# Cross-attention block: wholly masked queries through a 78th key, and four output projections as three f16 products

## The chip, the cores and the metric

The kernel runs on 1 core of one Trainium2 chip. The metric is the device time of one execution in microseconds (us); of several executions the median counts.

## The reference

Four sequences of 1024 queries attend to 77 context rows each, with 16 heads of 16 elements. Keys with mask 1 are excluded. The rest of the block is the output projection, the residual and a layer norm.

```python
q = split_heads(x @ W_Q.T); k = split_heads(ctx @ W_K.T); v = split_heads(ctx @ W_V.T)
scores = einsum('bhqd,bhkd->bhqk', q, k) / sqrt(16)
scores = where(mask[:, None] == 1, -1e9, scores)     # mask: (4, 1024, 77)
p = softmax(scores, axis=-1)
out = concat_heads(einsum('bhqk,bhkd->bhqd', p, v)) @ W_O.T + x
return (out - mean(out)) * rsqrt(var(out) + 1e-5) * gamma + beta
```

x is (4, 1024, 256), ctx (4, 77, 256), everything is f32 and the mask int32. Where all 77 keys of a query are masked, all scores are the same -1e9, so the softmax gives every key 1/77 and the query gets the mean of the values.

## The kernel before

**Tiles.** The 4096 queries are cut into 8 blocks of 512 (`BLOCKS`, `N`), two for each sequence. Columns hold queries. Heads go in 8 pairs; a block has 8 steps s = 0..7, one pair each. Each engine has its own program, all orders are written out by hand, and semaphores tie them.

**Scores as one matmul.** For block m the tile `R[m % 3]` has 126 partitions for each head: 77 rows of the mask (`eq16`: 61440 where the key is masked), 48 rows of q as f16 in three parts (high, low, high again), and one row with the negated maximum of the head. The tile `kb` holds the other side: a negated identity for the mask (`copy_tail`, L688), k in parts (high, high, low), and a row of ones. `scores` (L876) multiplies all 126 rows, two heads a step; `max_unit` (L845) multiplies the first 125 for the maxima, in 12 units a block (heads in groups of 6, 6 and 4, four tiles of 128 queries), which `reduce_max` (L631) reduces on DVE. `turn_max` transposes the 128x16 maxima on PE (L859), ACT copies them (L516) and a DMA (L520) writes them as one row of R. So the maxima of block n+1 are done in steps 0 to 3 of block n, those of n+2 are begun in steps 5 to 7 (`UNITS_LATE`, `UNITS_EARLY`); in block 0 units of blocks 0, 1 and 2 stand in the steps (`OWN_FIRST`, `NEXT_FIRST`, `EARLY_FIRST`).

**Wholly masked queries.** `count` (L804) sums the 77 mask rows of a block with one f16 matmul of ones into `work_ps`. ACT makes a flag of it (`nf`, L480: 1 if not all are masked, else 0), and `q_scale` (L620, DVE) multiplies the projected q by the flag on its way from PSUM into `q32`, so a wholly masked query has equal scores for all keys.

**q.** `project_q` (L824) projects a half of a block (128 of 256 outputs, 512 queries) in f32 into `work_ps`, at steps 1 and 3 of block n for block n+3. Then come `q_scale`, `q_hi` (L487, ACT: q as f16), `q_lo` (L344 on POOL; L613 on DVE for block 0: the rest as f16), and on SP `load_q` (L260 for the high part twice, L262 for the low part), which moves the halves into rows of R. `q_hi` waits until the previous block's parts have left `q16`. The mask comes as int32 by `load_mask_i`, becomes f16 by `eq` (L339 on POOL, L597 on DVE for blocks 0 and 1), and is spread over 8 heads by `load_mask` (L251, 616 KB for half of the heads); in blocks 0 and 1 DVE spreads it (L694).

**Values and output.** `exp` (L526, ACT) writes the probabilities of two heads. `values` (L885) multiplies four heads by v and by a column of ones, at steps 2, 4 and 6 and at step 0 of the next block. DVE turns the result (`turn`: L639, and the reciprocal of the sums, L641), POOL divides (`norm`, L351), DVE turns back (`turn_back`, L647). `project_out` (L895) projects in f32 the two halves of block n-1 at steps 5 and 7 of block n (steps 3 and 5 for n = 6), 4 matmuls a half, which the profile shows as 8 passes. DVE adds x (`residual`, L653), takes the statistics (L659, L664), POOL makes 1/std and the shift (`moments`, L360 to L365), ACT applies them (`apply`, L531) and POOL multiplies by gamma and adds beta (L372, L378). `work_ps`, one bank, serves count, project_q and project_out in turn; each waits for the reader of the one before.

**Orders around the change.** ACT at step 0: exp, nf(n+3); at 2 and 4: exp, q_hi(n+3); at step 4 (5 in block 0) turn_max(n+1) behind exp. DVE at step 2 and 4: q_scale(n+3), then reductions, turn, reductions. POOL in a block: norm, gamma and beta of block n-3, q_lo, moments(n-2), eq(n+4). SP in a pass n: mask and q of block n+2, second half; mask_i and x_t of block n+4; x; mask and q of block n+3, first half; the store of block n-3. SP waits in order, so each DMA of it is behind those before. w_o is loaded from ACT's queue behind q_hi(0, 0) (L547).

## Time and profile before

| what | value |
|---|---|
| median of 3 runs | 182.79 us (181.10 to 183.29) |
| the profiled execution's own time | 183.17 us |
| its span in the profile | 181.4 us |
| PE busy | 160.0 us (88%) |
| DVE busy | 136.5 us (75%) |
| ACT busy | 100.5 us (55%) |
| POOL busy | 95.8 us (53%) |
| mean granted TensorE clock | 0.988 |

The span is what lies between the first and the last instruction of the profiled execution; 1.8 us of its own time lie around it. Busy times count each engine's own instructions, which may overlap waits of others. Matmul ends are modelled, so two neighbouring PE rows can overlap by some 0.2 us; the distance of their starts is the better measure. The chain of waits goes back from the last instruction to what released it, step by step. Lines are those of the kernel before.

### The profile page before, as it was taken

The numbers are of one execution on the slowest core, as the hardware profiler recorded it, in microseconds if no ns is written. First come the engines' busy times: TensorE is split into PE (matmuls) and PEld (weight loads), VectorE is DVE, ScalarE is ACT, GpSimd is POOL, SyncE is SP. The second block draws the span as 40 slices with busy tenths as digits, with TensorE's granted clock in tenths as the row PEclk, the third lists the DMA queues.
The fourth block names the chain that finished last, engine by engine and source line by source line (L and its number), as shares of the span: only waits on it lengthen the run. The fifth ranks groups of instructions, "written<-read, shape, count | busy, mean of one in ns | idle before, by whom it ended". The sixth has DMA issues, their size and how long they took to land.

```text
span 181.4 us, 3507 instructions
## 1 busy us (share of the span) xinstructions
PE 160.0 (88%) x1224; PEld 87.0 (48%) x1224; DVE 136.5 (75%) x303; ACT 100.5 (55%) x134; POOL 95.8 (53%) x119
## 2 busy tenths in 40 slices
PE   7798878889699999999999999999899799799830
PEld 7555544343344554455545554554356364164520
DVE  0858757684978499778977897789989985758991
ACT  3224155563475655558755875586667458796400
POOL 7000750330743451249576957664954675895692
PEclk9999999999999999999999999999999999999995
DMA  5959958768767977872797575656541024011205
GB/s 174 350 144 169 260 86 222 208 143 246 195 173 239 268 223 222 266 195 48 212 264 188 179 209 133 190 159 197 148 173 64 4 107 129 0 59 61 116 0 231
DMA packets 21829, 30.17 MB, mean 166 GB/s; under 512 B 3436, under 2 KB 17356, under 8 KB 21812
## 3 DMA queue, kind: packets, MB, share of 16 engines
q1 hardware_dynamic: 20692, 28.19, 54.8%
q10 hardware_dynamic: 1120, 1.76, 2.9%
q8 instruction: 10, 0.16, 0.4%
q14 instruction: 7, 0.06, 0.1%
HBM read 11.28 MB, written 4.19 MB: 85 GB/s over the span
## 4 chain that ended last, share of the span: by engine, by line
PE 57%; DVE 11%; DMA 9%; issue 7%; POOL 7%; ACT 6%; SPq 1%; POOLq 0%; ACTq 0%; DVEq 0%
PE pv_ps L885 13%; PE work_ps L824 11%; PE work_ps L895 11%; PE scores_ps L876 9%; PE max_ps L845 8%; DMA x_t<-in_x_cols 4%; DVE neg_max L631 4%; DMA R<-neg_max_t 3%; DVE ctx_q L639 2%; DMA R<-q 2%; PE scores_ps L824 2%; POOL y L372 2%; ACT probs L526 2%; POOL y L378 1%; DVE first_max L631 1%
## 5 line engine op out<-in xcount | busy, mean ns | idle before, releaser
L526 ACT ACTIVATE probs<-scores_ps 77x1024 f32<-77x1024 f32 x60 | 60.5, 1017 | 43.7 <-PE scores_ps L876 38.4
L631 DVE TENSOR_REDUCE neg_max<-max_ps 128x6 f16<-128x462 f32 (+1 forms) x84 | 45.4, 565 | 11.9 <-PE max_ps L845 11.8
L845 PEld LDWEIGHTS max_ps<-kb,R 125*128 125x128 f16 x512 | 26.2, 98 | 34.4 <-DVE neg_max L631 17.8
L344 POOL TENSOR_TENSOR q<-q 128x512 f16<-128x512 f32 x14 | 16.2, 1155 | 49.5 <-ACT q L487 49.5
L876 PE MATMUL scores_ps<-R,kb 126*77 126x512 f16 x120 | 36.1, 384 | 1.0 <-DMA R<-neg_max_t 1.0
L845 PE MATMUL max_ps<-kb,R 125*128 125x77 f16 x512 | 31.9, 199 | 4.3 <-DVE neg_max L631 3.3
L885 PE MATMUL pv_ps<-probs,v_all 77*32 77x512 f32 x248 | 33.0, 604 | 2.6 <-ACT probs L526 1.5
L351 POOL TENSOR_TENSOR ctx_n<-ctx_q,rden 128x256 f32<-128x256 f32 x31 | 19.4, 627 | 23.9 <-DVE rden L641 23.6
L639 DVE STREAM_TRANSPOSE ctx_q<-pv_ps 128x512 f32<-128x512 f32 x31 | 22.0, 709 | 9.8 <-PE pv_ps L885 9.4
L895 PE MATMUL work_ps<-wo_t,ctx_e 128*128 128x256 f32 x112 | 27.0, 384 | 0.1
L824 PE MATMUL work_ps<-x_t,wq_t 128*128 128x512 f32 x48 | 23.6, 614 | 0.4
L895 PEld LDWEIGHTS work_ps<-wo_t,ctx_e 128*128 128x128 f32 x112 | 20.7, 190 | 3.6 <-issue 0.6
L372 POOL TENSOR_TENSOR y<-y,gamma_sb 128x512 f32<-128x512 f32 x14 | 17.8, 1272 | 3.0 <-ACT y L531 3.0
L531 ACT ACTIVATE y<-y,shift,rstd 128x256 f32<-128x256 f32 x28 | 15.1, 589 | 3.3 <-POOL shift L365 3.3
L378 POOL TENSOR_TENSOR y<-y,beta_sb 128x512 f32<-128x512 f32 x12 | 15.2, 1271 | 0.0
L876 PEld LDWEIGHTS scores_ps<-R,kb 126*77 126x77 f16 x120 | 9.9, 117 | 9.5 <-ACT probs L526 4.1
L487 ACT ACTIVATE q<-q 128x512 f16<-128x512 f32 x16 | 9.9, 620 | 7.5 <-DVE q L620 5.3
L339 POOL TENSOR_SCALAR eq<-mask_i 77x512 f16<-77x512 int32 x6 | 11.6, 1928 | 1.6 <-DMA mask_i<-in_mask_cols 1.2
L653 DVE TENSOR_TENSOR y<-work_ps,y 128x512 f32<-128x512 f32 x14 | 9.5, 680 | 2.7 <-PE work_ps L895 2.7
L647 DVE STREAM_TRANSPOSE ctx_e<-ctx_n 128x512 f32<-128x512 f32 x15 | 10.5, 701 | 1.1 <-POOL ctx_n L351 1.0
L824 PEld LDWEIGHTS work_ps<-x_t,wq_t 128*128 128x128 f32 x48 | 8.2, 190 | 6.6 <-issue 5.7
L659 DVE BATCH_NORM_STATS2 bn<-y 128x6 f32<-128x256 f32 x28 | 9.9, 397 | 0.0
(88 smaller groups left out, 149.0 us busy)
## 6 DMA issues: line engine op xcount, KB each, us to landing
R<-eq SPq DMA_DIRECT2D x12, 616.0 KB
R<-q SPq DMA_DIRECT2D x48, 128.0 KB
x_t<-in_x_cols SPq DMA_DIRECT2D x8, 512.0 KB, 5.4
y<-in_x SPq DMA_DIRECT2D x8, 512.0 KB, 4.6
out<-y SPq DMA_DIRECT2D x7, 512.0 KB, 2.6
mask_i<-in_mask_cols SPq DMA_DIRECT2D x8, 154.0 KB
out<-y ACTq DMA_DIRECT2D x2, 256.0 KB, 2.0
kb<-k SPq DMA_DIRECT2D x12, 38.5 KB, 2.9
```

The source lines that it names most:

```text
L344: nc.gpsimd.tensor_tensor(q16[:, e, 1, :], q32[:, e, :], q16[:, e, 0, :], ALU.subtract).then_inc(q_low, 1)
L351: nc.gpsimd.tensor_tensor(ctx_n[:, v, :, u * DK:(u + 1) * DK], ctx_q[:, t % 2, :, 0:DK], rden[:, t % 2, :].unsqueeze(2).to_broadcast([P, C ...
L372: nc.gpsimd.tensor_tensor(rows, rows, gamma_sb[:, :].unsqueeze(1).to_broadcast([P, 2, D]), ALU.mult).then_inc(y_gamma, 1)
L378: nc.gpsimd.tensor_tensor(rows, rows, beta_sb[:, :].unsqueeze(1).to_broadcast([P, 2, D]), ALU.add).then_inc(y_beta, 1)
L526: nc.scalar.activation(probs[:, s, :, :], scores_ps[scores_buffer(PAIRS * n + s)[0]][0:KEYS, :, :], ACT.Exp).then_inc(exp_done, 1)
L631: nc.vector.tensor_reduce(to[:, t, lo:hi], max_ps[u % 2][:, 0:(hi - lo) * KEYS].rearrange("p (h k) -> p h k", k=KEYS), AX.X, ALU.max, nega ...
L639: nc.vector.transpose(ctx_q[:, t % 2, :, :], pv_ps[:, :]).then_inc(pv_turned, 1)
L824: last = nc.tensor.matmul(bank, wq_t[:, t, e * P:(e + 1) * P], x_t[m % X_RING][:, t, :], start=(t == 0), stop=(t == HALVES - 1))
L845: last = nc.tensor.matmul(max_ps[u % 2][:, (h - lo) * KEYS:(h - lo + 1) * KEYS], R[m % R_RING][0:MAX_ROW, h, t * P:(t + 1) * P], kb[0:MAX_ ...
L876: last = nc.tensor.matmul(scores_ps[buffer][0:KEYS, i, :], kb[:, 2 * s + i, n // PER_BATCH, :], R[n % R_RING][:, 2 * s + i, :], start=True ...
L885: last = nc.tensor.matmul(pv_ps[32 * j:32 * (j + 1), :], v_all[:, n // PER_BATCH, 4 * t + j, :], probs[:, 2 * t + j // 2, j % 2, :], start ...
L895: last = nc.tensor.matmul(work_ps[:, i * D:(i + 1) * D], ctx_e[n % 2][:, v, q0:q0 + P], wo_t[:, v, :], start=(v == 0), stop=(v == HALVES - 1))
```

## The change

A 78th column of `kb` (`COLS = KEYS + 1`) stands for a key whose value is the mean of the values: its context row is the mean of the 77 others (`sum_ctx`, `mean_ctx` on DVE), so project_v gives its value. Its score comes from the mask's rows: each masked key adds 256, and a new row of R that is all ones (`ONE_ROW`) takes away 77 x 256 - 64. With all keys masked it stands 64 above zero, else at least 192 below. Its k is zero. The maxima are still taken over 77 keys. R and `kb` get 127 rows, exp writes 78 partitions.

- PE: the 8 counts go. project_q now waits for q_low (or out_ready) where it waited for the flag or q_scaled. project_v waits for ctx_mean. project_out of blocks 0 to 3 makes 12 f16 products a half (high x high, high x low, low x high for each of 2 halves of K and 2 tiles) instead of 4 f32 ones and waits for c_low instead of ctx_e_ready.
- ACT: the 8 flags go. q_hi reads PSUM as soon as q is projected, and stands before exp at steps 2 and 4 (2, 4, 6 in block 0; before exp(1, 0) for the last) instead of behind it. New: c_hi(n-1, v) behind exp at steps 0 and 2 of n = 1 to 4; w_hi behind exp(0, 5), ahead of turn_max(1). At the start ACT issues the high parts of k and q for the second half.
- DVE: q_scale goes; every q_lo comes here, reading PSUM, behind the first reductions of steps 2 and 4. New: sum_ctx, two mean_ctx, w_lo at step 7 of block 0, eq_late(n+4) at step 6 of n = 1 to 3 (ahead of the last reductions). residual multiplies by 1/64 for blocks 0 to 3 (w_o is scaled by 64). copy_tail copies a ready f16 tile.
- POOL: all q_lo go, and eq for blocks 5 to 7; eq(4) stands ahead of norm(0, 1). New: c_lo(n-1, v) for n = 1 to 4 behind norm(n-1, 3) and norm(n, 0); in blocks 1 to 4 beta and moments stand later; for block 6 norm(6, 0) moves ahead of both beta, and norm(6, 1) ahead of moments(4). Small memsets at the start.
- SP: w_o is loaded behind load_q(2, 1). At the start two rows of kb and the ones rows of R[0] and R[1] take the place of one row of ones; the ones row of R[2] goes behind the mask of block 2.

```diff
@@ PE
             def project_out(n, half):
                 if half == 0:
-                    pe.wait_ge(ctx_e_ready, HALVES * (n + 1))
+                    if n < OUT_SPLIT:
+                        pe.wait_ge(w_low, 1)
+                        pe.wait_ge(c_low, HALVES * (n + 1))
+                    else:
+                        pe.wait_ge(ctx_e_ready, HALVES * (n + 1))
...
+                        if n < OUT_SPLIT:
+                            for of_c, of_w in [(0, 0), (0, 1), (1, 0)]:
+                                last = nc.tensor.matmul(work_ps[:, i * D:(i + 1) * D], c16[:, v, of_c, q0:q0 + P], wo16[:, of_w, v, :],
+                                                        start=(v == 0 and of_c + of_w == 0), stop=(v == HALVES - 1 and of_c == 1))
...
                     if 1 <= n and n + 3 < N:
-                        if s == 0:
+                        if s == 1:
                             if n >= 2:
                                 pe.wait_ge(out_ready, 2 * (n - 1))
                             else:
-                                pe.wait_ge(q_scaled, 4 * HALVES)
-                            count(n + 3)
-                        if s == 1:
-                            pe.wait_ge(nf_ready, n + 4)
+                                pe.wait_ge(q_low, 4 * HALVES)
                             project_q(n + 3, 0, work_ps[:, :])
                         if s == 3:
-                            pe.wait_ge(q_scaled, HALVES * (n + 3) + 1)
+                            pe.wait_ge(q_low, HALVES * (n + 3) + 1)
                             project_q(n + 3, 1, work_ps[:, :])
@@ ACT
-            def q_hi(m, e):
-                act.wait_ge(q_scaled, HALVES * m + e + 1)
+            def q_hi(m, e, bank):
+                act.wait_ge(q_done, HALVES * m + e + 1)
                 if m > 0:
                     act.wait_ge(s_R[(m - 1) % R_RING][e], loaded_R(m - 1))
-                nc.scalar.activation(q16[:, e, 0, :], q32[:, e, :], ACT.Copy).then_inc(q_high, 1)
+                nc.scalar.activation(q16[:, e, 0, :], bank, ACT.Copy).then_inc(q_high, 1)
+
+            def c_hi(m, v):
+                act.wait_ge(ctx_e_ready, HALVES * m + v + 1)
+                if m > 0:
+                    act.wait_ge(out_done, 2 * m)
+                nc.scalar.activation(c16[:, v, 0, :], ctx_e[m % 2][:, v, :], ACT.Copy).then_inc(c_high, 1)
+
+            def w_hi(w16, w_t, s_w):
+                act.wait_ge(s_w, 16)
+                nc.scalar.activation(w16[:, 0, :, :], w_t[:, :, :], ACT.Copy, scale=WSCALE).then_inc(w_high, 1)
...
             for n in range(N):
                 for s in range(STEPS):
+                    if n == 0 and s in (2, 4, 6):
+                        q_hi(2 + s // 6, s // 2 - 1 if s < 6 else 0, work_ps[:, :])
+                    if n == 1 and s == 0:
+                        q_hi(3, 1, work_ps[:, :])
+                    if n >= 1 and n + 3 < N and s in (2, 4):
+                        q_hi(n + 3, s // 2 - 1, work_ps[:, :])
                     exp(n, s)
                     if n == 0:
                         if s == 1:
                             turn_first_max(2)
-                        if s in (2, 4, 6):
-                            q_hi(2 + s // 6, s // 2 - 1 if s < 6 else 0)
-                        if s == 4:
-                            nf(3)
+                        if s == 5:
+                            w_hi(wo16, wo_t, s_wo)
...
                     if s == nm_at(n) and n + 1 < N:
                         turn_max(n + 1)
@@ DVE
+            def eq_late(m):
+                dve.wait_ge(s_mask[m % 2], 16 * (m // 2 + 1))
+                for e in range(HALVES):
+                    dve.wait_ge(s_R[(m - 2) % R_RING][e], loaded_R(m - 2))
+                nc.vector.tensor_scalar(eq16[m % 2][:, :], mask_i[m % 2][:, :], 1.0, BIG, ALU.is_equal, ALU.mult
+                                        ).then_inc(eq_ready, 1)
...
                     for m, u in before:
                         reduce_max(m, u)
+                    if n == 0 and s in (2, 4, 6):
+                        q_lo(2 + s // 6, s // 2 - 1 if s < 6 else 0, work_ps[:, :])
+                    if n >= 1 and n + 3 < N and s in (2, 4):
+                        q_lo(n + 3, s // 2 - 1, work_ps[:, :])
+                    if n == 0 and s == 7:
+                        w_lo(0, wo16, wo_t)
                     if s == 0 and n >= 1:
                         turn(n - 1, 3)
                     if s in (2, 4, 6):
                         turn(n, s // 2 - 1)
...
+                    if s == 6 and 1 <= n and n + 4 < N:
+                        eq_late(n + 4)
                     for m, u in behind:
                         reduce_max(m, u)
@@ POOL
             norm(N - 3, 3)
             times_gamma(N - 5, 1)
+            norm(N - 2, 0)
             plus_beta(N - 5, 0)
-            norm(N - 2, 0)
             plus_beta(N - 5, 1)
+            norm(N - 2, 1)
             moments(N - 4)
-            norm(N - 2, 1)
             times_gamma(N - 4, 0)
```

## Rows read from the trace of the kernel before

**Rows 1.** Busy time of each engine, from the page (share of the span, instructions)

```profile
PE 160.0 (88%) x1224; PEld 87.0 (48%) x1224; DVE 136.5 (75%) x303; ACT 100.5 (55%) x134; POOL 95.8 (53%) x119
```

**Rows 2.** Windows of two middle blocks: stretch, length, busy us (instructions), clock, DMA, GB/s

```profile
69.40:87.70 18.30, 18.08 (x145) 9.60 (x142) 15.29 (x35) 12.20 (x17) 9.49 (x12) 1.00 0.64 181
87.70:106.00 18.30, 18.08 (x147) 9.62 (x145) 15.30 (x36) 12.22 (x17) 13.28 (x16) 1.00 0.74 209
```

**Rows 3.** Chain of waits, one out projection and what follows: start us, us

```profile
61.78 1.73 PE work_ps L895 x8
63.51 0.23 PE max_ps L845 x6
...
66.16 0.43 PE scores_ps L876 x2
```

**Rows 4.** Chain of waits, count, flag and projection of q in block 2

```profile
70.47 0.34 PE work_ps L804
70.83 0.69 ACT not_full L480
71.57 1.98 PE work_ps L824 x4
```

**Rows 5.** Groups by line and form: count, busy us, mean ns, idle before

```profile
L344 POOL TENSOR_TENSOR q<-q 128x512 f16<-128x512 f32 x14 | 16.2, 1155 | 49.5 <-ACT q L487 49.5
...
L487 ACT ACTIVATE q<-q 128x512 f16<-128x512 f32 x16 | 9.9, 620 | 7.5 <-DVE q L620 5.3 <-DMA R<-q 2.2
...
L620 DVE TENSOR_TENSOR q<-work_ps,not_full 128x512 f32<-128x512 f32 x12 | 8.2, 684 | 1.3 <-PE work_ps L824 1.3
...
L597 DVE TENSOR_SCALAR eq<-mask_i 77x512 f16<-77x512 int32 x2 | 0.8, 418 | 3.4 <-DMA mask_i<-in_mask_cols 3.4
```

**Rows 6.** DVE in order of time: start us, us, idle time before it

```profile
82.06 1.18 DVE L631 TENSOR_REDUCE neg_max<-max_ps 128x6 f16<-128x462 f32 x2 [0.85 <-PE max_ps L845]
```

**Rows 7.** DMA issues: KB each, median us from issue to landing

```profile
wq_t<-in_w_q ACTq DMA_DIRECT2D x1, 256.0 KB, 4.9
...
wo_t<-in_w_o ACTq DMA_DIRECT2D x1, 256.0 KB, 2.6
...
R<-neg_max_t ACTq DMA_DIRECT2D x7, 16.0 KB, 4.7
...
kb<-ones SPq DMA_DIRECT2D x1, 9.6 KB, 7.6
```

**Rows 8.** A DVE copy (ns min/median/max) and a POOL norm beside it

```profile
L688 DVE TENSOR_SCALAR kb<-ident x4: 473/474/798, 4.6 to 47.1; 77x1232 f16<-77x1232 f16 x4
...
47.50 0.86 POOL L351 TENSOR_TENSOR ctx_n<-ctx_q,rden 128x256 f32<-128x256 f32 x1
```

**Rows 9.** Chain of waits at the start: the third DMA of q

```profile
13.06 3.89 DMA R<-q
```

**Rows 10.** Block 0 in order of time, then two pieces of its chain

```profile
31.86 0.61 ACTq L510 DMA_DIRECT2D R<-first_max_t  x1
...
33.02 0.72 DVE L639 STREAM_TRANSPOSE ctx_q<-pv_ps 128x512 f32<-128x512 f32 x1 [0.88 <-PE pv_ps L885]
...
40.30 0.61 SPq L262 DMA_DIRECT2D R<-q  x1
...
43.55 0.59 ACT neg_max_t L516
44.16 5.91 DMA R<-neg_max_t
```

**Rows 11.** The end of block 6 in order of time

```profile
147.73 0.23 POOL L360 TENSOR_SCALAR var_eps<-mean_var 128x4 f32<-128x4 f32 x1
...
149.76 0.62 POOL L351 TENSOR_TENSOR ctx_n<-ctx_q,rden 128x256 f32<-128x256 f32 x1
...
151.01 1.08 ACT L531 ACTIVATE y<-y,shift,rstd 128x256 f32<-128x256 f32 x2
...
154.94 1.07 PE L885 MATMUL pv_ps<-probs,v_all 77*32 77x512 f32 x8 [1.00 <-ACT probs L526]
```

More of the change, by code:

```diff
@@ L30 @@
 CHUNKS = BLOCK // 32
+COLS = KEYS + 1
 Q_ROW = KEYS
 MAX_ROW = Q_ROW + 3 * DK
-ROWS = MAX_ROW + 1
-MASKED = 61440.0
+ONE_ROW = MAX_ROW + 1
+ROWS = ONE_ROW + 1
+BIG = 32768.0
+PER_KEY = 256.0
+WHOLE = 64.0
 KSCALE = 1.0 / float(DK) ** 0.5
@@ L305, in _ @@
                     load_q(n + 2, 1)
+                if n == 0:
+                    sp.dma_start(wo_t[:, :, :], w_o).then_inc(s_wo, 16)
                 if n == 1:
@@ L332, in eq, with c_lo @@
                 pool.wait_ge(s_mask[m % 2], 16 * (m // 2 + 1))
-                pool.wait_ge(count_done, m - 1)
                 if m - 2 < SPREAD:
                     pool.wait_ge(first_mask, HALVES * (m - 1))
-                else:
-                    for e in range(HALVES):
-                        pool.wait_ge(s_R[(m - 2) % R_RING][e], loaded_R(m - 2))
-                nc.gpsimd.tensor_scalar(eq16[m % 2][:, :], mask_i[m % 2][:, :], 1.0, MASKED, ALU.is_equal, ALU.mult
+                nc.gpsimd.tensor_scalar(eq16[m % 2][:, :], mask_i[m % 2][:, :], 1.0, BIG, ALU.is_equal, ALU.mult
                                         ).then_inc(eq_ready, 1)
-            def q_lo(m, e):
-                pool.wait_ge(q_high, HALVES * m + e + 1)
-                nc.gpsimd.tensor_tensor(q16[:, e, 1, :], q32[:, e, :], q16[:, e, 0, :], ALU.subtract).then_inc(q_low, 1)
+            def c_lo(m, v):
+                pool.wait_ge(c_high, HALVES * m + v + 1)
+                nc.gpsimd.tensor_tensor(c16[:, v, 1, :], ctx_e[m % 2][:, v, :], c16[:, v, 0, :], ALU.subtract).then_inc(c_low, 1)
             def norm(m, t):
@@ L705, in _ @@
             spread_mask(0, 1)
-            q_scale(0, 0, q_ps[0][0])
+            sum_ctx()
+            mean_ctx(0)
+            q_lo(0, 0, q_ps[0][0])
             eq(1)
-            q_lo(0, 0)
-            q_scale(0, 1, q_ps[0][1])
-            q_lo(0, 1)
+            q_lo(0, 1, q_ps[0][1])
             spread_mask(1, 0)
-            q_scale(1, 0, q_ps[1][0])
             spread_mask(1, 1)
             k_lo_second()
-            for u in range(TILES):
-                reduce_max(0, u)
+            mean_ctx(1)
+            reduce_max(0, 0)
+            reduce_max(0, 1)
+            q_lo(1, 0, q_ps[1][0])
+            reduce_max(0, 2)
+            reduce_max(0, 3)
             reduce_max(0, TILES)
             reduce_max(0, TILES + 1)
-            q_scale(1, 1, q_ps[1][1])
             reduce_max(0, TILES + 2)
+            q_lo(1, 1, q_ps[1][1])
             reduce_max(0, TILES + 3)
@@ L732, in _ @@
                     if n == 1 and s == 0:
-                        q_scale(3, 1, work_ps[:, :])
+                        q_lo(3, 1, work_ps[:, :])
                     if s == 0 and n >= 2:
                         residual(n - 2, 1)
-                    if s in (2, 4) and 1 <= n and n + 3 < N:
-                        q_scale(n + 3, s // 2 - 1, work_ps[:, :])
                     if s == 6 and 1 <= n < N - 2:
@@ L801, in _ @@
         def _(pe):
-            def count(m):
-                pe.wait_ge(eq_ready, m + 1)
-                nc.tensor.matmul(work_ps[:, :], ones16[:, :], eq16[m % 2][:, :], start=True, stop=True).then_inc(count_done, 1)
             def project_k(p, e):
@@ L936, in _ @@
             max_unit(0, 7)
-            pe.wait_ge(v_ready, 2)
-            count(2)
             pe.wait_ge(first_ready, 1)
             turn_first_max(1)
-            pe.wait_ge(q_scaled, HALVES)
-            pe.wait_ge(tail_ones, 16)
+            pe.wait_ge(q_low, HALVES)
+            pe.wait_ge(s_last_rows, 64)
             for n in range(N - 1):
```

221 lines of the change are left out of this document (116 added, 105 removed).

## The prediction

> **What bounds the kernel now.** I read the page first: PE is busy 88% of the span and DVE 75% [rows 1], of a span of 181.4 us with 1.8 around it. Then the windows of two middle blocks: each takes 18.30 us, PE busy 18.08 of it at a granted clock of 1.00, DVE 15.3, ACT 12.2, POOL 9.5 to 13.3 [rows 2]. So blocks 2 to 4 are bound by TensorE at its full 2.4 GHz, and DVE has 3 us to spare. Then the chain of waits, for the places where PE is not the last link: the start (x_t, q and q's way into R), block 0 (ACT, DVE, and the row of maxima on its way to R) and the end (moments, apply, exponentials). A shorter PE stage pays in the middle; moved work can cost at both ends. Below, n is the block of a loop pass, s its step.
>
> **Middle: out projections.** A half has 8 recorded f32 passes of 256 columns, 1.73 us [rows 3]. It gets 12 f16 products of 256 columns. The nearest rows: two f16 scores of 512 columns in 0.43 us, 0.215 each, and six maxima, each with 128 columns of new weights, in 0.23 [rows 3]. So the weights hide, 256 columns cost 0.107, and 12 cost 1.28. Gain 0.45 a half, 0.9 a block, in four blocks (n = 1 to 4). Bounds: 0.7 a block if each product pays 0.01 more, 1.0 if what follows an f32 half starts a little sooner behind an f16 one.
>
> **Middle: count and flags.** Each block's chain holds the count (0.34 with its latency) and ACT's flag (0.69) before project_q starts at 71.57, 1.10 after the count [rows 4]. In that time PE also runs two scores and a unit, 0.43 + 0.22 by rows 3. That leaves 0.45 to 0.5, of which 0.21 is the count's own 512 columns; I take 0.47. Three times (n = 2 to 4) 1.4; n = 1, where ACT was in time, is counted below.
>
> **What must fit around it.** DVE trades two q_scale (0.68) for two q_lo of the same kind, tensor_tensor on PSUM, and adds eq_late for n = 1 to 3, 0.42 as at the start [rows 5]. 15.3 + 0.4 = 15.7, against a new period of 18.30 - 1.37 = 16.9: it fits, narrowly. Walking one period: the first maximum is reduced at 82.06, 0.4 after its unit starts, two in 1.18 [rows 6]; reductions follow 0.55 apart, residual takes 0.6, turn 0.9, turn_back 0.65. Counted from that unit, DVE reduces at 0.4 and 1.0, residual from 1.5, reduces, turns until 3.6, eq_late until 4.0, reduces twice, turns back until 5.75 and reduces again until 6.3, with no gap. PE, shorter by one half, waits 0.05 for a reduction there and another 0.1 in the next step, and the old DVE gap of 0.85 before 82.06 [rows 6] takes up the rest. ACT loses a flag and gains two c_hi of q_hi's size, 0.62 [rows 5]. POOL loses two q_lo (1.15 [rows 5]) and eq and gains two c_lo of the same size; the second, behind norm(n,0), ends 1.6 us before PE asks for it. Moments come 1.3 us later in a block, apply holds the next exponential 0.7, and values still find theirs. The row of maxima gets 5.7 us instead of 6.6, and its median landing is 4.7 [rows 7]. PE's new waits on q_low end 0.2 and 0.7 us before it arrives. Middle: 4 x 0.9 + 1.4 = 5.0 less.
>
> How a DVE copy and POOL meet is in two rows: the last of the four identity copies, at 47.1, took 0.80 against a median of 0.47, and the POOL norm at 47.50 beside it 0.86 [rows 8], where the one of rows 11 takes 0.62. In the Trainium skill, "SBUF — State Buffer", section "Who interferes with whom", GpSimd and a copy or tensor_scalar in a 2-port mode hold one port pair in turn for a whole instruction; by that rule, the trace agrees. It speaks against eq_late, which would wait for POOL's instruction, or hold back the norm that starts with it, in three blocks in which DVE is just full. What it would cost by rows stands in the first rival.
>
> **Start.** q_hi no longer waits for q_scale (0.68), and half of the q and k DMAs go out on ACT's queue, so block 0's first half lands about 0.8 before the 16.95 of now (13.06 + 3.89 [rows 9]). But project_k(1) keeps PE until 16.6, sum_ctx and mean_ctx come onto DVE, and q_lo(1,0) and q_lo(1,1), once on POOL, stand between reductions; q_hi(1,1) is behind an ACT DMA issue and v_copy. I get scores(0,0) 0.4 earlier (bounds: 1.3 earlier, 0.7 later). SP issues four more small DMAs, 0.6 each, ahead of mask_i(2), but eq(2) is wanted only at 28.0; at the 7.6 us of the row of ones [rows 7] the new rows land by 24.1, in time.
>
> **Block 0, q_lo(2,0).** ACT issues the last group's maxima until 32.47 (31.86 + 0.61) and only then does q_hi(2,0), 0.62. q_lo(2,0) stands before turn(0,0), now at 33.02 [rows 10]. With everything 0.4 earlier: q_hi to 32.7, q_lo to 33.4, so the turn comes 0.8 late, and the chain runs through it, the next reduction and the unit at 34.66. q_scale's old place was beside a gap and gives nothing back. +0.75 (bounds 0.2 to 0.9).
>
> **Block 0, w_o.** Its load moves from ACT at 11.18 to SP, behind load_q(2,1), whose last issue is at 40.30 [rows 10]; new about 40.4. w_hi waits for it on ACT ahead of turn_max(1), now at 43.55; behind that stand the DMA of the maxima (5.91 us [rows 10]), q_hi(3,0), for which q_lo and DVE's turn(0,2) wait, and exp(0,6). 256 KB landed in 2.6 us in a quieter stretch and 4.9 in a full one [rows 7]: between 43.0 and 45.3. I take 43.8. The shift so far is +0.35, so turn_max would start at 43.9; with w_hi until 44.45 it starts at 44.5, and its DMA at 45.1, behind 256 KB more: landing 51.0 to 51.2 instead of 50.07. The other path gives the same: q_hi(3,0) to 46.3, q_lo to 47.0, turn to 47.9, a reduction, project_q(3,1) from 48.75, a unit to 50.8. So scores(1,0) is 1.1 late, +0.8 more (bounds 0 to +2.3). By project_q at n = 1 PE has 0.4 back: no count, and w_lo (0.69) and q_lo(3,1) on DVE hold a unit only a little. eq(4) on POOL waits for R(2) and mask_i(4), some 46, ahead of norm(0,1), which turn_back(0,0) wants at 50.7: 2 us in hand.
>
> **End.** For n = 6 moments(4) moves behind norm(6,1). It now starts at 147.73; norm(6,1), which waits for its turn, starts at 149.76 [rows 11]. The four steps of moments take 1.94 (147.73 to 149.67, just ahead of the norm), so the new shift is ready at 149.76 + 0.62 + 1.94 = 152.3, and ACT's apply, now at 151.01, waits for it. Two exponentials stand behind it, and values(6,3) at 154.94 was already waiting 1.00 for the second [rows 11]. +1.35 (bounds 0.5 to 1.5). Nothing later takes it back.
>
> **Sum.** -0.4 + 0.75 + 0.8 - 0.4 - 5.0 + 1.35 = -2.9. On the profiled execution's 183.17 that is 180.3. It lies 0.4 above the median, 182.79, from which the same sum gives 179.9. I say 180.1.
>
> **Rivals.**
> - DVE takes over the middle. For it: 15.7 of 16.9 us, and eq_late, which by rows 8 could be 0.33 longer (the copy's loss), up to 1.15 (a whole POOL instruction of q_lo's size). Against: the walk finds waits of 0.05 to 0.1. With 0.55 lost in each of four blocks: 182.3.
> - The costs at the ends stay away: w_o lands before 43.3, the start gives 1.0, q_lo(2,0) costs 0.3. That is 0.6 + 0.6 + 0.45 better: 178.5. For it: the landing of 2.6. Against: it goes out behind three q DMAs.
> - Slower: w_o holds ACT ahead of turn_max(1). Each us by which it lands after 43.8 costs one. From 46.7, 6.3 us after its issue, the kernel is slower than before; at 7.6 us, the longest landing of this trace, 184.3. Against: the masks and x of the next block are issued behind it.
> - The change doesn't do what it says: f16 products as slow as the passes. 12 x 0.216 = 2.6 a half, 0.86 more instead of 0.47 less: 190. Rows 3 speak against it.
>
> **How the numbers follow.** Forecast 0.42, DVE 0.20, ends free 0.28, w_o late 0.09, slow products 0.01. Two per cent is 3.7 us, about what a measurement of this kernel can tell from no change. Faster (under 179.1): the third case and a seventh of the first, 0.34. Slower (over 186.4): 0.07, of the w_o case with a second stall behind it and the slow products. Within: 0.59. Range 177.2 to 183.8: from the start's and w_o's better bounds together to the w_o case.
>
> **What would show it.** From project_q to project_q 16.9 us in the middle instead of 18.3, twelve products in 1.3 us a half; w_hi ending near 44.5 and the maxima's DMA issued near 45; turn(0,0) behind a waiting q_lo; at the end apply waiting for shift and values(6,3) idle over 2 us. Wrong: a period above 17.6 with units waiting for reductions in steps 6 and 7 (DVE), w_hi starting before 42, or scores(0,0) later than 26.3.

## The result: 1.3% slower, not faster

| what | kernel before | changed kernel |
|---|---|---|
| median beside each other | 183.04 us (4 runs, 181.10 to 186.94) | 185.10 us (4 runs, 184.57 to 185.70) |
| ratio, 95% interval | | 1.0127 [1.0081, 1.0173] |
| once more, later (e9) | 183.63 us (30 runs) | 184.64 us (12 runs) |
| ratio, 95% interval | | 1.0057 [1.0012, 1.0102] |
| profiled execution, span | 183.17, 181.4 us | 185.70, 183.9 us |
| mean granted TensorE clock, profiled | 0.988 | 0.961 |

The forecast was 180.1 with a range from 177.2 to 183.8, and 0.59 on "within 2%". Twice the kernel came out slower, by less than 2%, and the first median lies above the range. Ratios compare the undisturbed executions of both kernels on one chip, while medians count all of them, so the two need not agree.

The page of the changed kernel, busy time and granted clock by slices (one digit is a fortieth of the span, tenths of full speed):

```profile
PE 157.9 (86%) x1248; PEld 84.8 (46%) x1248; DVE 136.8 (74%) x308; ACT 100.8 (55%) x135; POOL 84.7 (46%) x116
...
PEclk9999999999969999999999999999999999589995
```

PE has 2.1 us less to do than in [rows 1], yet the span is 2.5 longer. The second line shows two dents which the prediction did not speak of: slice 12 and slices 35 and 36 (a slice is 4.6 us; the low last slice, in which PE has finished, stands in the page of the kernel before too). The windows that go with them (length, busy us of PE, PEld, DVE, ACT, POOL with counts, clock, DMA share, GB/s):

```profile
74.01:90.87 16.86, 16.77 (x150) 8.73 (x149) 15.28 (x36) 12.90 (x18) 7.72 (x11) 1.00 0.72 197
90.87:107.72 16.85, 16.76 (x149) 8.72 (x149) 15.28 (x36) 12.34 (x17) 11.41 (x14) 1.00 0.80 226
45.00:50.40 5.40, 1.38 (x18) 0.57 (x14) 2.10 (x5) 3.52 (x5) 2.96 (x3) 0.97 0.78 176
50.99:54.10 3.11, 3.11 (x10) 1.24 (x11) 2.07 (x4) 0.00 (x0) 0.00 (x0) 0.60 0.81 178
152.00:157.00 5.00, 2.76 (x13) 0.51 (x12) 2.48 (x8) 4.74 (x7) 4.36 (x4) 0.89 0.16 65
157.00:163.00 6.00, 6.00 (x20) 3.29 (x20) 2.55 (x8) 3.02 (x4) 5.09 (x8) 0.53 0.04 14
```

The first two answer to [rows 2]: a middle block takes 16.86 and 16.85 us where it took 18.30, PE is busy 16.77 of it, DVE 15.28, the clock is full. The other four come in pairs, a stretch in which PE mostly waits (1.38 busy of 5.40; 2.76 of 5.00) and behind it one in which PE is busy all the time at a mean clock of 0.60 and 0.53, that is, four fifths and nearly all of it at 1.2 GHz instead of 2.4. In the kernel before PE is busy 3.71 us of the stretch 45.00 to 50.40 and 3.62 us of 152.00 to 157.00, and the clock is 1.00 in both and in the stretches behind them.

Block 0 in order of time: SP's issue of w_o, then ACT, then PE.

```profile
40.32 0.59 SPq L344 DMA_DIRECT2D wo_t<-in_w_o  x1
...
45.85 0.63 ACT L520 ACTIVATE wo<-wo_t 128x512 f16<-128x512 f32 x1 [4.76 <-DMA wo_t<-in_w_o]
46.39 0.57 ACT L549 ACTIVATE neg_max_t<-max_ps 16x512 f16<-16x512 f16 x1
...
47.10 0.59 PE L899 MATMUL max_ps<-kb,R 125*128 125x77 f16 x12 [1.74 <-ACT neg_max_t L549]
...
50.42 0.57 PE L899 MATMUL max_ps<-kb,R 125*128 125x77 f16 x6 [2.30 <-DVE neg_max L682]
50.79 3.29 PE L878 MATMUL work_ps<-x_t,wq_t 128*128 128x512 f32 x4
```

w_o lands 5.5 us after its issue, not 3.4. w_hi has ACT wait 4.76 for it, and turn_max(1)'s copy starts at 46.39 instead of 43.55 [rows 10]. PE waits 1.74 and 2.30 for what hangs on that copy. Then project_q(3,1) takes 3.29 us instead of 1.96, four matmuls of the same form.

The end of block 6, on POOL, ACT and PE:

```profile
149.06 0.23 POOL L395 TENSOR_SCALAR var_eps<-mean_var 128x4 f32<-128x4 f32 x1
...
151.03 1.09 ACT L564 ACTIVATE y<-y,shift,rstd 128x256 f32<-128x256 f32 x2 [1.32 <-POOL shift L400]
...
153.09 0.62 PE L932 MATMUL max_ps<-R,kb 127*78 127x512 f16 x2 [0.97 <-ACT probs L559]
154.97 1.11 PE L941 MATMUL pv_ps<-probs,v_all 78*32 78x512 f32 x8 [1.26 <-ACT probs L559]
...
157.02 1.93 PE L941 MATMUL pv_ps<-probs,v_all 78*32 78x512 f32 x8
...
159.75 3.35 PE L960 MATMUL work_ps<-wo_t,ctx_e 128*128 128x256 f32 x8
...
163.46 1.06 PE L941 MATMUL pv_ps<-probs,v_all 78*32 78x512 f32 x8
```

Against [rows 11]: apply waits 1.32 for the shift, and PE has two waits, 0.97 and 1.26, where there was one of 1.00. After it values(7,0) takes 1.93 instead of 1.07, and project_out 3.35 instead of about 1.97.

**The ledger** of the two profiled executions, by the starts of the same instruction, both taken from the chain of waits or both from the timeline (on PE the two differ by up to 0.2). scores(0,0): 26.42 to 25.82, -0.6. turn_max(1) on PE: 43.12 to 43.42, +0.3. project_q(4,0): 53.13 to 56.91, +3.8. project_q(5,0): 71.57 to 74.01, +2.4. project_q(7,0): 108.14 to 107.72, -0.4. values(4,3): 124.28 to 122.73, -1.6. values(6,3): 154.94 to 154.97, 0.0. values(7,1): 161.00 to 163.46, +2.5. So by stage: start -0.6, block 0 +4.4, middle from its first block on -5.4, end +4.1, together the +2.5 of the spans.

### The profile page after: what moved, and what is told of

Same layout as the page of the kernel before. It is cut to its first block, busy times and chain, and to the rows that moved or that the text cites. A ratio compares the mean times of both kernels' runs of the same rounds, so it can differ in the third digit from the quotient of the medians.

```text
span 183.9 us, 3537 instructions
## 1 busy us (share of the span) xinstructions
PE 157.9 (86%) x1248; PEld 84.8 (46%) x1248; DVE 136.8 (74%) x308; ACT 100.8 (55%) x135; POOL 84.7 (46%) x116
## 3 DMA queue, kind: packets, MB, share of 16 engines
q10 hardware_dynamic: 1552, 1.84, 3.7%
## 4 chain that ended last, share of the span: by engine, by line
PE 59%; DVE 13%; POOL 7%; DMA 7%; issue 6%; ACT 4%; SPq 1%; ACTq 1%; POOLq 0%; DVEq 0%
PE pv_ps L941 13%; PE work_ps L878 11%; PE scores_ps L932 10%; PE max_ps L899 8%; DVE neg_max L682 5%; PE work_ps L957 5%; PE work_ps L960 5%; PE scores_ps L878 4%; DMA x_t<-in_x_cols 4%; DMA wo_t<-in_w_o 3%; DVE ctx_q L690 2%; POOL y L407 2%; DVE first_max L682 2%; DVE q L649 1%; POOL y L413 1%
## 5 line engine op out<-in xcount | busy, mean ns | idle before, releaser
L559 ACT ACTIVATE probs<-scores_ps 78x1024 f32<-78x1024 f32 x60 | 60.2, 1016 | 23.3 <-PE scores_ps L932 19.1
L932 PE MATMUL scores_ps<-R,kb 127*78 127x512 f16 x120 | 37.0, 392 | 0.0
L941 PE MATMUL pv_ps<-probs,v_all 78*32 78x512 f32 x248 | 33.9, 620 | 2.5 <-ACT probs L559 1.8
L510 ACT ACTIVATE q<-work_ps 128x512 f16<-128x512 f32 x12 | 7.2, 597 | 15.5 <-PE work_ps L878 14.1
L649 DVE TENSOR_TENSOR q<-work_ps,q 128x512 f16<-128x512 f32 x12 | 8.2, 685 | 9.4 <-ACT q L510 9.3
L932 PEld LDWEIGHTS scores_ps<-R,kb 127*78 127x78 f16 x120 | 9.7, 117 | 11.4 <-ACT probs L559 5.8
L960 PE MATMUL work_ps<-wo_t,ctx_e 128*128 128x256 f32 x48 | 13.0, 418 | 0.0
L704 DVE SCALAR_TENSOR_TENSOR y<-work_ps,y 128x512 f32<-128x512 f32 x14 | 9.5, 677 | 4.6 <-PE work_ps L960 4.6
L957 PE MATMUL work_ps<-wo,c 128*128 128x256 f16 x96 | 11.8, 272 | 0.0
L960 PEld LDWEIGHTS work_ps<-wo_t,ctx_e 128*128 128x128 f32 x48 | 10.1, 214 | 2.0 <-issue 0.2
```

The costliest lines, as they stand in the source:

```text
L559: nc.scalar.activation(probs[:, s, :, :], scores_ps[scores_buffer(PAIRS * n + s)[0]][0:COLS, :, :], ACT.Exp).then_inc(exp_done, 1)
L932: last = nc.tensor.matmul(scores_ps[buffer][0:COLS, i, :], kb[:, 2 * s + i, n // PER_BATCH, :], R[n % R_RING][:, 2 * s + i, :], start=True ...
L941: last = nc.tensor.matmul(pv_ps[32 * j:32 * (j + 1), :], v_all[:, n // PER_BATCH, 4 * t + j, :], probs[:, 2 * t + j // 2, j % 2, :], start ...
L957: last = nc.tensor.matmul(work_ps[:, i * D:(i + 1) * D], c16[:, v, of_c, q0:q0 + P], wo16[:, of_w, v, :], start=(v == 0 and of_c + of_w == ...
L960: last = nc.tensor.matmul(work_ps[:, i * D:(i + 1) * D], ctx_e[n % 2][:, v, q0:q0 + P], wo_t[:, v, :], start=(v == 0), stop=(v == HALVES - 1))
```

## The experiments

**Theory.** Two things cost more than forecast: w_o's landing, and the granted clock, which falls behind long waits of PE and makes what follows longer (1.93 us instead of 1.07, 3.35 instead of 1.97). **Rivals.** The waits alone explain the loss; the f16 products or DVE fail to give what the middle should. The first four kernels undo one part or two.

**e1: w_o's load back on ACT's queue.**

```diff
             q_hi(0, 0, q_ps[0][0])
+            act.dma_start(wo_t[:, :, :], w_o).then_inc(s_wo, 16)
...
-                if n == 0:
-                    sp.dma_start(wo_t[:, :, :], w_o).then_inc(s_wo, 16)
```

> Changed kernel with the load of w_o back on ACT's queue behind q_hi(0,0). Theory (ACT waits for w_o ahead of turn_max(1), PE idles, and its clock falls after that): w_hi starts right behind exp(0,5), near 41.1; turn_max(1) near 43.9 instead of 46.39; scores(1,0) near 50.5 instead of 54.13; project_q(3,1) takes 1.8 us instead of 3.1, clock 1.00 there; time 3.5 us below the changed kernel's 185.1, 181.6. The end stays as it is, low clock included. Rival (q_lo and q_hi ahead of turn and exp are the larger stall, w_o only part of it): scores(1,0) not before 52, less than 2 us gained, the low clock stays.

Measured: median 185.14 of 10 runs, ratio 0.990 [0.9838, 0.9963]. Its profiled execution took 526.7 us, for a reason that isn't known (each projection of q took 6.9 us there at a granted clock of 1.00), so its trace can't be compared. What is left is the list of times: 180.8 and 181.8 at clocks of 0.977 and 0.978, 182.3 at 0.968, and six from 184.1 to 186.6 at 0.949 to 0.963. The kernel can reach the time expected, 181.6, but mostly doesn't. That is inconclusive for w_o alone, and a first sign that the clock decides: these nine executions of one program differ by 5.8 us.

**e2: moments(4) ahead of norm(6,1) again.**

```diff
-            norm(N - 2, 1)
             moments(N - 4)
+            norm(N - 2, 1)
```

> Changed kernel with moments(4) back ahead of norm(6,1). Theory (apply waits 1.3 for shift, the exponentials behind it starve PE, and PE's clock falls from 156 to 163): the wait goes, values(6,3) 1.4 earlier against values(6,2), and the clock stays 1.00 there: 1.4 + 2.4 = 3.8 less, 181.3. Rival (the low clock at the end has another cause, say the stall in block 0 or the f16 products): only 1.4 less, 183.7, with projections of 3.1 us still in the end.

Measured: 180.97 (4 runs), ratio 0.978 [0.9682, 0.9879]. PE at the end of block 6:

```profile
151.71 1.07 PE L941 MATMUL pv_ps<-probs,v_all 78*32 78x512 f32 x8 [1.00 <-ACT probs L559]
...
155.44 1.97 PE L960 MATMUL work_ps<-wo_t,ctx_e 128*128 128x256 f32 x8
```

One wait of 1.00 as before the change, and project_out at full speed. The moved moments cost a wait, forecast at 1.35, and where the clock falls behind it more. But part of this run's gain is not its own: here w_o landed 3.0 us after its issue instead of 5.5 (its program is the same up to there), and project_q(3,1) took 1.95. And one fall came elsewhere: behind a wait of 1.80 at the start, project_q(2,0) took 2.93 instead of 1.96.

**e3: both undone.**

> Both edits, the early load of w_o and moments(4) ahead of norm(6,1). Theory (two separate stalls, each with its own clock fall): the gains add, 3.5 + 3.8 = 7.3, 177.8, 5 us below the kernel before, since the middle's 5.0 is then all kept. Rival (one common cause behind both): 3.5 to 4 in all, 181.3.

Measured: 181.0 (4 runs), ratio 0.9848 [0.9768, 0.9927]; no better than e2. Against e1, from which it differs by the place of moments(4) alone, its four executions (179.3 to 181.7) lie below eight of e1's nine (180.8 to 186.6), and that is the better evidence for what this place is worth. In its trace nothing waits for w_o, and still:

```profile
50.00 0.43 PE L898 MATMUL max_ps<-kb,R 125*128 125x77 f16 x6 [1.57 <-DVE neg_max L681]
50.22 3.65 PE L877 MATMUL work_ps<-x_t,wq_t 128*128 128x512 f32 x4
```

project_q(3,1) takes 3.65 behind a wait of 1.57. At the start, behind a wait of 1.98, scores(0,0) and the matmuls after it took 1.04 instead of 0.60 as well. So the fall doesn't need w_o's late landing: a wait of 1.57 is enough in some executions (0.65 in the kernel before, at the same place). That the places of q_lo and w_hi on DVE and ACT make this wait longer is argued from the order, not shown by a run of its own. My additive expectation of 177.8 failed on that.

**e4: w_hi behind exp(0, 7), its load still on SP, w_lo in block 1.**

```diff
-                        if s == 5:
+                        if s == 7:
                             w_hi(wo16, wo_t, s_wo)
...
-                    if n == 0 and s == 7:
+                    if n == 1 and s == 2:
                         w_lo(0, wo16, wo_t)
```

> Changed kernel with w_o loaded on SP as it is, but w_hi behind exp(0,7) instead of exp(0,5), and w_lo at step 2 of block 1. Theory (the order on ACT is what costs, not the load): turn_max(1) near 43.9, scores(1,0) near 50.7, project_q(3,1) at full clock, about 3.3 less: 181.8, as with the early load. Rival (w_o's 256 KB in the DMA queue hold back the row of maxima and the mask): maxima land at 51.5 or later, scores(1,0) at 51.7 or later, 2 us less at most: 183.

Measured: 183.52 (10 runs), ratio 1.0001 [0.9952, 1.005]; the profiled one 181.58 at a clock of 0.987. Its rows on ACT and on PE, in block 0 and at the end:

```profile
43.78 0.59 ACT L549 ACTIVATE neg_max_t<-max_ps 16x512 f16<-16x512 f16 x1 [2.76 <-PE max_ps L913]
...
48.06 1.95 PE L878 MATMUL work_ps<-x_t,wq_t 128*128 128x512 f32 x4
...
151.41 0.62 PE L932 MATMUL max_ps<-R,kb 127*78 127x512 f16 x2 [0.97 <-ACT probs L559]
153.30 1.06 PE L941 MATMUL pv_ps<-probs,v_all 78*32 78x512 f32 x8 [1.26 <-ACT probs L559]
...
159.36 1.06 PE L941 MATMUL pv_ps<-probs,v_all 78*32 78x512 f32 x8
```

The median misses the 181.8 expected by 1.7. With w_hi out of the way turn_max(1)'s copy is at 43.78, 2.6 us earlier than in the changed kernel, so w_hi is what held it. The end is the cleanest comparison of this case: the same two waits, 0.97 and 1.26, as in the changed kernel, but here the clock stayed, and from values(6,3) to values(7,1) it takes 6.06 us (153.30 to 159.36) against 8.49 (154.97 to 163.46). The fall at the end costs 2.43 (in the trace of e9, the same program as the changed kernel, the same stretch takes 8.59). Whether it comes differs between executions of the same waits: of the other nine executions of e4, two have clocks of 0.981 and 0.978 and take 181.5 and 182.8 us, seven have 0.967 or less and take 183.1 to 184.3.

**Does the idle PE cause the falls?** The next kernels leave every wait of the data alone and give PE products of zeros in them, whose results are written over. They aren't free: they go into `pv_ps`, so that in two of the three places PE waits until DVE has turned what stood there, and what is not done when the data come holds PE up.

**e5: e3 with 30 such products ahead of turn_first_max(1), 16 in step 7 of block 0.**

```diff
             pe.wait_ge(first_ready, 1)
+            for _ in range(30):
+                nc.tensor.matmul(pv_ps[:, 0:P], zeros16[:, :], zeros16[:, :], start=True, stop=True)
             turn_first_max(1)
...
+                    if n == 0 and s == 7:
+                        pe.wait_ge(pv_turned, 3)
+                        for _ in range(16):
+                            nc.tensor.matmul(pv_ps[:, 0:P], zeros16[:, :], zeros16[:, :], start=True, stop=True)
```

> e3 with 46 products of zeros on TensorE in two of its waits, 30 of 128 columns ahead of turn_first_max(1) and 16 ahead of max_unit(2, 2) in step 7 of block 0 (their results are written over). Nothing is waited for less: DVE and ACT give the same semaphores at the same times. Theory (the granted clock falls to its lower level after these two waits, and project_q(2, 0) and project_q(3, 1) then take 2.4 to 3.7 us instead of 1.95): both take 1.8 to 2.0 us in the profile, the clock of the span is 0.985 or more, and the time is 2 to 3 us under that of e3, 178 to 179 us. Rival (the clock falls from another cause than an idle TensorE, or the time is lost behind the same releases anyway): clock 0.96 to 0.975 and time as e3, 180.5 to 181.5.

Measured: 180.04 (6 runs, 178.76 to 182.91), ratio 0.9842 [0.978, 0.9903]. Its page, and the wait for the row of maxima, on PE and in the chain:

```profile
PEclk9999999999999999999999999999999999999995
```

```profile
69.66 0.62 PE L931 MATMUL scores_ps<-R,kb 127*78 127x512 f16 x2 [1.50 <-DMA R<-neg_max_t]
```

```profile
62.12 7.50 DMA R<-neg_max_t
```

The clock is full in every slice but the last, and both project_q took 1.95 and 1.96. Four of six executions have 0.986 to 0.993, where those of e3 have 0.972, 0.972, 0.978 and 0.986. The time fell by 1.0 only, not 2 to 3; the ratio hardly differs from that of e3. One reason is in the other two rows: block 1 is entered 3.4 us earlier than in the changed kernel (project_q(4,0) at 53.32 against 56.75), but block 2 only 1.75 (project_q(5,0) at 72.10 against 73.85), because scores(2,0) waits 1.50 for the row of maxima, which takes 7.50 to land. In the changed kernel the row is issued at 65.55 and scores(2,0) finds it at 71.43, within 5.9 us, without a wait. The DMA engines are busier while the row of e5 is on its way, a share of 0.79 against 0.60. (The expectation of e12 calls this matmul scores(1,7); by the program and the order of the rows it is scores(2,0).)

**e6: the changed kernel with 32 zero products at the end alone.**

```diff
             scores(n, 0)
+            pe.wait_ge(pv_turned, QUADS * (n - 1) + 3)
+            for _ in range(16):
+                nc.tensor.matmul(pv_ps[:, 0:P], zeros16[:, :], zeros16[:, :], start=True, stop=True)
             scores(n, 1)
...
             values(n - 1, 3)
```

> The changed kernel with 32 products of zeros (128 columns each, written over) around scores(7, 0) and scores(7, 1), ahead of values(6, 3); moments(4) stays behind norm(6, 1), so apply waits for the shift as before and values(6, 3) starts no earlier. Theory (at the end the change costs 1.4 us of wait and then 1 to 2.5 us of low clock): project_out behind it takes 1.75 to 2.0 us instead of 3.35, the clock there is 1.00, and the time is 1 to 2.4 us under that of the changed kernel. Rival (the loss at the end is the wait for the moved moments alone): the same time as the changed kernel within 0.5 us.

Measured: 181.44 (7 runs), ratio 0.9896 [0.9827, 0.9965], 3.7 under the first median of the changed kernel and 3.2 under the one of e9, neither measured beside it; somewhat more than expected, and w_o landed after 4.1 us in its trace, not 5.5.

```profile
155.01 1.07 PE L941 MATMUL pv_ps<-probs,v_all 78*32 78x512 f32 x8 [0.37 <-ACT probs L559]
...
158.74 1.97 PE L960 MATMUL work_ps<-wo_t,ctx_e 128*128 128x256 f32 x8
...
161.07 1.06 PE L941 MATMUL pv_ps<-probs,v_all 78*32 78x512 f32 x8
```

values(6,3) starts at 155.01, as late as in the changed kernel (154.97), since apply still waits for the shift. But project_out takes 1.97, and values(7,1) follows after 6.06 us instead of 8.49. The theory holds for the end, in the size e4 gave, and the rival, the wait for the moments alone, is out. In block 0, where no zeros stand, its clock fell again (project_q(3,1) 3.76 us).

**e7: e3 without the f16 split, the 78th key kept** (`OUT_SPLIT = 0`, no w_hi, w_lo, c_hi, c_lo).

> e3 with the out projections of blocks 0 to 3 in f32 again: OUT_SPLIT = 0, no w_hi, w_lo, c_hi, c_lo. The 78th key stays. Theory (each half gains 0.42 us on TensorE, which bounds the middle): the distance of project_q(n+3, 0) rises from 16.86 to 17.7 (16.86 plus 2 x 0.42), four blocks cost 3.4 us, and with no w_hi ahead of turn_max(1) about 0.5 comes back in block 0: 183.5 to 184.5 us if the clock falls as often as in e3. Rival (DVE, full with q_lo and eq_late, bounds the middle at 16.86 and the products gain little): distance below 17.3 and 182 us or less.

Measured: 184.75 (12 runs), ratio 1.0049 [1.0002, 1.0097]. Two middle blocks of it, columns as above:

```profile
74.64:92.40 17.76, 17.67 (x145) 9.43 (x142) 15.46 (x36) 11.77 (x16) 5.50 (x9) 1.00 0.64 186
92.40:110.16 17.76, 17.67 (x145) 9.43 (x142) 15.49 (x36) 11.78 (x16) 9.19 (x12) 1.00 0.77 215
```

17.76 against 16.86 with the products: 0.90 a block, my 2 x 0.45. And 17.76 against the 18.30 of [rows 2]: 0.54 for count and flag and all else that the change moved in a middle block, where I had put 0.47. The rival of a DVE-bound middle is out. The split pays for itself, and without it the 78th key has not made the kernel faster.

**e8: e3 with q_lo(1, 1) behind the last first maximum and q_lo(3, 0) behind turn(0, 2).**

> e3 with two q_lo of DVE moved behind the work that TensorE waits for: q_lo(1, 1) behind the last reduction of first maxima, q_lo(3, 0) behind turn(0, 2). Theory (these stand in front of what TensorE waits for, 0.5 to 0.7 us each, and the longer waits cost the clock): the wait ahead of turn_first_max(1) is 1.2 us again instead of 1.8 to 2.0, scores(0, 0) starts 0.5 us earlier, project_q(2, 0) takes 1.95 us, and the time is 1 to 2 us under that of e3, 179 to 180. Rival (what follows waits for R by DMA or for q_low, so the order on DVE is worth nothing): as e3 within 0.5 us.

Measured: median 182.9 (6 runs, 179.57 to 185.25), ratio 0.9877 [0.9796, 0.9958]. In the profile the wait ahead of turn_first_max(1) is 1.16, scores(0,0) starts at 24.87 instead of 26.46 in e3, and project_q(2,0) and (3,1) take 1.96 and 1.95, as expected. But the gain is taken at other places: 1.22 and 1.88 us of waiting for the next two rows of maxima (scores(1,0), scores(2,0)), and a fall of the clock at the end, where project_out takes 2.30 behind waits of 1.00 and 0.38. The order of DVE works as read; the total isn't measurably better than e3's.

**e9: the changed kernel again, beside e10 to e12.**

> The changed kernel once more, unaltered, beside the next three on one chip. Theory (two things vary between executions: how long w_o takes to land, and whether the granted clock falls after the long waits of TensorE): its executions spread over more than those of the kernel before, from about 182.5 (clock 0.975 or more) to 186 (clock 0.95), and the time goes with the clock, about 1.2 us for each 0.01. Rival (the change is slower by its waits alone): all within 184.5 to 185.7 as in the first measurement, whatever the clock.

Measured: 184.64 (12 runs, 182.54 to 189.75), clocks 0.941 to 0.977, and the fastest is the one at 0.977. In the profiled execution w_o took 6.6 us to land:

```profile
46.47 0.63 ACT L520 ACTIVATE wo<-wo_t 128x512 f16<-128x512 f32 x1 [5.81 <-DMA wo_t<-in_w_o]
```

Both parts of the theory are seen to vary: landings of 3.0, 4.0, 4.1, 5.5, 6.6 and 6.6 us in six traces with this load on SP, against 2.6 to 3.2 in the seven where ACT issues it early; and the clock. From 182.5 at 0.977 to 186.5 at 0.953 it is 1.6 us for each 0.01, more than the 1.2 I wrote down; and 0.961 alone goes with 183.4 to 185.5, so something besides the clock moves the time, as a varying landing would. By and large the landing goes with how busy the DMA engines are meanwhile: their share between issue and landing is 0.67, 0.83, 0.84 and 0.97 for 3.0, 4.0, 4.1 and 5.5 us, and, as the profile prints it, 1.02 and 0.94 for the two of 6.6, against 0.62 for the early load of the kernel before. In each of the six SP issues mask_i, x_t and half of a spread mask (154, 512 and 616 KB) within 1.6 us behind w_o.

**e10: the changed kernel with zeros in three waits** (30 ahead of turn_first_max(1), 30 in step 7 of block 0, 32 at the end).

> The changed kernel with 92 products of zeros (128 columns each, written over) in three waits of TensorE: 30 ahead of turn_first_max(1), 30 ahead of max_unit(2, 2) in step 7 of block 0, 32 around the scores of block 7 ahead of values(6, 3). w_o stays on SP and moments(4) behind norm(6, 1): every wait of the change stays as long. Theory (loss = waits plus what the clock costs behind them): clock 0.985 or more, project_q(3, 1) and the project_out of block 6 at full speed (1.96 and 1.75), 180.5 to 181.5 us, that is 2.5 to 4 us under the changed kernel on the same chip. Rival (waits alone): as the changed kernel within 1 us.

Measured: 182.14 (12 runs), ratio 0.9924 [0.9877, 0.9971], clocks 0.985 to 0.994 in ten of twelve. Against e9 on the same chip that is 2.5 us less, with every wait of the change still in it. The two intervals don't touch, and the rival, waits alone, is out. The profiled execution is the longest of the twelve, 186.25 us, and shows the limit of the means: w_o had landed late again (6.6), PE had waited 2.81 just ahead, and the zeros themselves ran at half speed.

```profile
48.08 0.58 PE L899 MATMUL max_ps<-kb,R 125*128 125x77 f16 x12 [2.81 <-ACT neg_max_t L549]
...
50.62 3.38 PE L1014 MATMUL pv_ps<-zeros 128*128 128x128 f16 x30 [1.52 <-DVE ctx_q L690]
```

Thirty products in 3.38, where those at the start of e5 took 1.84.

**e11: the kernel before with 78 zero products in the same places.**

> The kernel before with the products of zeros of e5 and e6: 30 ahead of turn_first_max(1), 16 in step 7 of block 0, 32 ahead of values(6, 3). Theory (the waits before the change are short enough for the clock to stay, mean 0.988): within 0.7 us of the kernel before, clock 0.985 to 0.994. Rival (TensorE loses clock in the kernel before too, and the products help any kernel): 1.5 us or more under it.

Measured: 184.23 (12 runs), ratio 1.0068 [1.0034, 1.0102], clocks 0.986 to 0.995. On the whole the zeros cost the kernel before 0.6. But it is not free of the falls, and here the theory is too simple: 11 of the 30 executions of the kernel before on this chip have clocks of 0.960 to 0.983 and take 183.9 to 188.4 us, while none of the twelve of e11 is below 0.986. The zeros take the falls away here too; against the other 19, whose median is 182.9, they cost 1.3. What the change did is to make the rule of what was the exception: all twelve executions of e9 have 0.977 or less. With the clock kept, at 0.985 or more, the median of the changed kernel with zeros is 181.9 (10 executions of e10), 1.0 under the 182.9 of the kernel before, and the zeros' own cost is still in it.

**e12: all that helped together** (e3, e4's places for w_hi and w_lo, e8's order, zeros in three waits).

> All that helped together: w_o loaded from ACT's queue behind q_hi(0, 0), w_hi behind exp(0, 7) and w_lo at step 2 of block 1, moments(4) ahead of norm(6, 1), q_lo(1, 1) and q_lo(3, 0) behind what TensorE waits for, and 78 products of zeros in three waits. Theory: clock 0.985 or more, scores(0, 0) at 25.3, no wait for w_o anywhere, scores(1, 0) near 49.5 and its DMA of maxima issued 0.6 earlier than in e8; the next row of maxima, which in e5 and e8 held scores(1, 7) for 1.5 to 1.9 us, still holds it for 1 to 2 us: 178 to 179 us. Rival (the rows of maxima take all of it back): as e5, 180.

Measured: 180.01 (6 runs, 179.22 to 182.13), ratio 0.9825 [0.977, 0.9879], beside 184.64 for the changed kernel on that chip. scores(0,0) at 25.43, project_q(3,1) at 47.45, and then the row of maxima, issued at 61.25:

```profile
61.25 7.53 DMA R<-neg_max_t
```

```profile
68.82 0.62 PE L933 MATMUL scores_ps<-R,kb 127*78 127x512 f16 x2 [1.53 <-DMA R<-neg_max_t]
...
72.05 2.80 PE L879 MATMUL work_ps<-x_t,wq_t 128*128 128x512 f32 x4
```

It beats both kernels, the one before by 3.6 us; e5 and e2 do so about as well. It is not the 178 to 179 expected: the row of maxima takes back part of what block 0 gives (the wait of 1.53 is again that of scores(2,0)), and behind it the clock fell once more in this execution.

## Why the prediction was wrong

- **Middle: right.** Period 16.9 forecast, 16.86 and 16.85 measured. Twelve products take 1.31 in the chain where I had 1.28, e7 gives 0.90 a block for them and 0.54 for count and flag. DVE is busy 15.28 of 16.86; the rival that it takes over had 0.20. eq_late with POOL beside it cost nothing that the period shows: it takes 0.36, and the one POOL norm that I looked at beside it 0.68 instead of 0.62, where rows 8 had let me fear 0.33 or more.
- **Start: right.** scores(0,0) 0.6 earlier against 0.4.
- **q_lo(2,0) in block 0: right, at its upper bound.** DVE waits 1.41 for q_hi(2,0) and makes q_lo at 32.62; from scores(0,0) to turn_max(1) the shift goes from -0.6 to +0.3, so 0.9 against +0.75 (bounds 0.2 to 0.9).
- **w_o: the mechanism right, the term mis-sized.** The step is "I take 43.8" for the landing, between 43.0 and 45.3. It landed at 45.83, 0.5 beyond the bound, in the first trace and later still in e9. By my own rule, one us for each us after 43.8, +0.8 becomes +2.8, and with the 0.4 that PE has back by project_q(4,0) +2.4. The ledger has 3.5 from turn_max(1) to project_q(4,0), of which 1.3 is clock, so 2.2. I gave the case 0.09, although one of the two 256 KB landings in [rows 7] had taken 4.9. My argument against it, that the masks and x are issued behind w_o, did not keep it short: they are issued within 1.6 us, while w_o is still on its way.
- **End: right in size.** apply waits for the shift, values(6,3) is late by 1.6 against the 1.35 forecast (-1.6 before it, 0.0 at it); the "idle over 2 us" shows as two waits, 0.97 and 1.26.
- **The step that failed for the sign: every sum priced a wait of PE by its length alone, and put what follows it, the granted clock, at nothing without a reason.** "Nothing later takes it back" is true of the 1.35 at the end, but what came behind it was a further loss. In the profiled execution the fall of the clock costs 1.3 us in block 0 (project_q(3,1) 3.09 instead of 1.79 in the chain) and 2.4 at the end. With it the account closes: -2.9 forecast, +2.0 for w_o and +3.7 for the clock give +2.8, and the spans differ by +2.5. Without the 3.7 the ledger would end at -1.2, at 182.0: inside the range, though above the forecast. That is an estimate, and e5 and e12 show that not all of what block 0 wins reaches the end. I had read clocks of 1.00 in the middle [rows 2] and never asked what the clock does after a wait. The page of before gave no hint, since its line of the clock is the one shown for e5, low in the last slice alone, and its three executions lay within 2.2 us. The later ones do: with 30 executions, a third has falls and takes up to 188.4 us.
- **Small slips of the sum.** The lower end of the range doesn't follow from its words: the better bounds of the start and of w_o together give 178.4, not 177.2. Nor does the upper: the w_o case gives 181.6 at its bound of +2.3 and 184.3 at the longest landing, not 183.8. The case of the slow products sets its 0.86 against 0.47 where the gain of a half was 0.45. None of these decides anything here.

What is shown: that the fall costs 2.4 at the end (e4 and e6 against the changed kernel, same end of the program), that filling the waits brings back 2.5 of the whole (e10 against e9), that filling them in the kernel before brings nothing on the whole, since it has the falls in a third of its executions only (e11), and that moments(4) is worth its place (e3 against e1; e2). What stays open: why one execution keeps the clock behind the same waits and another doesn't; why w_o lands after 3.0 us in one execution and 6.6 in another (it goes with the DMA share while it is on its way, 0.67 to 1.02, but what fills the engines was not changed alone); and how much of e1 is w_o.

On the first of these, the Trainium skill, "TensorE: Matmul & The Clock Gate", section "What's actually happening", says that the gate judges recent activity at a phase that doesn't start with the kernel, so that the place of a change of clock varies from run to run. The traces fit that: e3 and e4 have the same wait of 1.57 ahead of project_q(3,1), which then took 3.65 in one and 1.95 in the other. No run here could set that phase.

## What to carry to other kernels

Price a wait of TensorE twice: by its length, and by what follows it at half the clock if the clock falls; here that was 1.3 to 2.4 us for waits of 1 to 2.3 us that stood near one another, and it came in some executions and not in others. So in a kernel that TensorE bounds, an edit that moves waits together on a stage with little matmul work can cost more than it removes elsewhere, even where each wait looks small. Put a load whose landing varies where nobody stands in line behind its reader: w_hi two steps later had no wait of its own on ACT and freed turn_max(1) by 2.6 us.
